# A perceiver block on one core: the first stage's tiles in a new order

## The reference, cut to what matters

```python
x = x + xattn0(layernorm(x), ctx)      # (gelu_tanh(xn ctx^T) * (xn ctx^T)) ctx
x = x + attn0(layernorm(x))            # qkv; RMS norm of q and k per head; rotation; causal softmax, 16 heads of 32
x = x + experts(layernorm(x))          # 32 experts, top 2 of a softmax, capacity 77, hidden 2048
x = x + xattn1(layernorm(x), ctx)      # 16 heads over 257 keys
x = x + attn1(layernorm(x))            # decayed attention, group norms, silu feed-forward
x = x + spectral(layernorm(x))         # fft -> product with w -> real ifft, + bias

def _rms_norm(t, w):
    return t * rsqrt(mean(t * t) + EPS) * w
# _rope(q, k): [q1*cos - q2*sin, q2*cos + q1*sin] of the normed q and k
```

## Time and profile before

| | us |
|---|---|
| runs, median of 3 | 2064.54 (2060.41 to 2065.12) |
| the profiled execution: time | 2075.67 |
| its span | 2073.9 |
| PE busy | 1934.6 (93%) |
| DVE, ACT, POOL busy | 704.7, 556.9, 196.9 |
| mean granted clock of TensorE | 0.97 |
| first stage with its routing, to the experts' first product | 336.55 |

### The profile page before, as it was taken

The page is one execution under the profiler, slowest core; times in us unless marked ns, Lnnn a source line. Parts: engine busy times, 40 slices in busy tenths (PEclk is TensorE's granted clock), DMA queues, the critical chain, the costliest instruction groups (busy, mean ns, idle before and its releaser), DMA issues.

```text
span 2073.9 us, 37462 instructions
## 1 busy us (share of the span) xinstructions
PE 1934.6 (93%) x15676; PEld 981.9 (47%) x15676; DVE 704.7 (34%) x1536; ACT 556.9 (27%) x1123; POOL 196.9 (9%) x182
## 2 busy tenths in 40 slices
PE   5789777999999999999996999999999999999977
PEld 2444453333333333333333657565666656575543
DVE  2666671121111211112223433434323333344323
ACT  1333311222222222222211234233333333242321
POOL 1122221000000000000003000000000000000000
PEclk9999988999999999999998999999999999999988
DMA  9643228999999999999976020100000000000000
GB/s 338 221 163 144 79 73 344 396 396 387 382 388 375 380 362 379 379 375 379 367 280 207 22 102 22 27 21 27 12 26 22 21 27 22 17 22 27 11 1 11
DMA packets 86295, 374.95 MB, mean 181 GB/s; under 512 B 7782, under 2 KB 25702, under 8 KB 53432
## 3 DMA queue, kind: packets, MB, share of 16 engines
q1 hardware_dynamic: 79544, 355.71, 44.9%
q0 software_dynamic: 6656, 17.77, 2.4%
HBM read 357.73 MB, written 16.45 MB: 180 GB/s over the span
## 4 chain that ended last, share of the span: by engine, by line
PE 85%; issue 4%; ACT 3%; SPq 3%; DMA 2%; DVE 2%; POOL 1%; another core or an unknown queue 0%; POOLq 0%; DVEq 0%; ACTq 0%
PE ps L1323 38%; PE ps L1506 16%; PE ps L1488 16%; PE ps L1713 3%; PE ps L1496 2%; PE ps L1608 1%; PE ps L1514 1%; DMA arena<-in_ctxT 1%; ACT arena L685 1%; PE ps L1384 1%; PE ps L1593 1%; DMA xe_rows<-arena,uidx 1%; PE ps L1634 1%; SPq L432 1%; PE ps L1477 1%
## 5 line engine op out<-in xcount | busy, mean ns | idle before, releaser
L1323 PE MATMUL ps<-arena 128*128 128x512 f32 (+3 forms) x3120 | 893.6, 442 | 38.0 <-ACT arena L685 10.0
L1323 PEld LDWEIGHTS ps<-arena 128*128 128x128 f32 x3120 | 529.1, 193 | 372.6 <-issue 296.7
L1506 PE MATMUL ps<-arena 128*32 128x512 f32 x3072 | 373.6, 594 | 0.0
L1488 PE MATMUL ps<-arena 128*32 128x512 f32 x3072 | 363.3, 595 | 0.7 <-issue 0.6
L550 POOL TENSOR_TENSOR arena<-arena 128x1 f32<-128x1 f32 (+3 forms) x80 | 129.2, 1615 | 1103.2 <-DVE arena L913 643.7
L1121 DVE COPY arena<-ps 128x512 f32<-128x512 f32 x96 | 66.4, 691 | 482.7 <-PE ps L1506 482.7
L1488 PEld LDWEIGHTS ps<-arena 128*32 128x32 f32 x3072 | 109.3, 109 | 225.4 <-issue 225.4
L1506 PEld LDWEIGHTS ps<-arena 128*32 128x32 f32 x3072 | 100.4, 109 | 198.1 <-issue 195.6
L783 ACT ACTIVATE arena<-ps 128x512 f32<-128x512 f32 x96 | 57.3, 597 | 352.5 <-PE ps L1488 352.5
L813 ACT ACTIVATE arena<-ps,arena 128x257 f32<-128x257 f32 x128 | 60.7, 477 | 202.8 <-PE ps L1323 202.8
L1220 DVE TENSOR_REDUCE arena<-ps 128x1 f32<-128x257 f32 x128 | 54.2, 423 | 122.5 <-PE ps L1593 112.7
(11 more groups left out here) (198 smaller groups left out, 1323.8 us busy)
## 6 DMA issues: line engine op xcount, KB each, us to landing
arena<-in_w SPq DMA_DIRECT2D x64, 4096.0 KB, 13.8
arena<-in_ctxT SPq DMA_DIRECT2D x8, 2056.0 KB, 7.9
arena<-in_ctxT SPq DMA_DIRECT2D x32, 514.0 KB, 3.6
arena<-in_ctx SPq DMA_DIRECT2D x8, 2048.0 KB
xe_rows<-arena SPq DMA_DIRECT2D x8, 616.0 KB
arena<-in_b POOLq DMA_DIRECT2D x32, 154.0 KB, 7.5
arena<-xe_rows SPq DMA_DIRECT2D x32, 154.0 KB
y_rows<-arena POOLq DMA_DIRECT2D x32, 154.0 KB, 6.2
```

The lines of the kernel that those rows point to most:

```text
L1323: ins = pe.matmul(dst, lhsT, rhs, start=(n == 0), stop=(n == len(pairs) - 1))
L1488: ins = pe.matmul(ps[q4[n], t, :], xeT[s][:, k, q4[t]], w1_sb[s][:, k, n * D:(n + 1) * D], start=(k == 0), stop=(k == KD - 1))
L1506: ins = pe.matmul(ps[q4[n], ST + t, :], hT[s][:, t, c, q4[n]], w2_sb[s][:, n * HB + c, :], start=(c == 0), stop=(c == HB - 1))
```

## The change

A new piece generator, `lead(i)` (letter h), takes norm 0 and its transposes and copy out of `gated(i)`; it runs two tiles ahead of `scored` and one ahead of `gated`, and tile 1's stands ahead of `scored(0)`. Norm 1 is cut into `moments` and `normed`, in two pieces. On DVE the rotation reads the products in PSUM (banks 4 and 5) and is multiplied by the root afterwards (into qkr); the buffer qkn now holds the rotated values. On PE the QKV product is issued values first, then a `yield`, then queries and keys; the scores move from `scored(i)` to the first piece of `attended(i)`, so that they stand in the next turn between its value product and its query and key products. The transposed queries and keys now lie in banks 4 and 5, the scores in bank 3 (6 for the last tile, function bA), transposes of xn and the logits in bank 3 (7 for the last two, bR). The loop runs over i = 2 to 5 and tile 6's turn is written out behind it. The folds are cut in halves, one behind the last rotation, one ahead of the last softmax. The pieces of ACT and POOL follow. Line numbers here are those of the changed kernel where the order rows show them.

```diff
 
-        PLAN_A = "gzawgawgzgagzaga"
-        PLAN_B = "zwwrmrzzrm"
+        PLAN_A = "hazagawzgawgzagazh"
+        PLAN_B = "wzwrmrzzzrm"
         CUT = NT - 2
...
             if isinstance(i, int) and i == tile:
                 eng.wait_ge(s, value)
 
+        def bA(i):
+            return 6 if isinstance(i, int) and i == NT - 1 else 3
+
+        def bR(i):
+            return 7 if isinstance(i, int) and i >= NT - 2 else 3
+
         def counts_at(part):
             a, b = BATCHES[part]
             return 2 * a * E, (a + b) * E, 2 * b * E
 
-        def phase_a(eng, gated, scored, attended, routed, spectral, my, per, route):
-
+        def phase_a(eng, lead, gated, scored, attended, routed, spectral, my, per, route):
+
+            run(lead(0))
             run(gated(0))
-            interleave(PLAN_A, a=scored(0), g=gated(1))
-            interleave(PLAN_A, a=scored(1), g=gated(2), z=attended(0))
-            with eng.Fori(2, NT - 1) as i:
+            run(lead(1))
+            interleave(PLAN_A, a=scored(0), g=gated(1), h=lead(2))
+            interleave(PLAN_A, a=scored(1), g=gated(2), h=lead(3), z=attended(0))
+            with eng.Fori(2, NT - 2) as i:
                 if my is not None:
                     my.loop(i, per, 2)
-                interleave(PLAN_A, a=scored(i), g=gated(i + 1), z=attended(i - 1), w=routed(i - 2))
+                interleave(PLAN_A, a=scored(i), g=gated(i + 1), h=lead(i + 2), z=attended(i - 1), w=routed(i - 2))
             if my is not None:
-                my.leave(NT - 1)
+                my.leave(NT - 2)
+            interleave(PLAN_A, a=scored(NT - 2), g=gated(NT - 1), z=attended(NT - 3), w=routed(NT - 4))
             interleave(PLAN_A, a=scored(NT - 1), z=attended(NT - 2), w=routed(NT - 3))
             interleave(PLAN_B, z=attended(NT - 1), w=routed(NT - 2), m=spectral, r=route(0))
             run(routed(NT - 1))
...
             def norm_root(a, n):
                 root(veps, rstd, ln_stats[a], n + 1, ln_rstd[a])
 
+            def lead(i):
+                norm_root(0, i)
+                yield
+                yield
+
             def gated(i):
-                norm_root(0, i)
-                yield
-                yield
                 yield
                 yield
                 norm_root(1, i)
...
             def bc(ap, *shape):
                 return ap.broadcast_to(list(shape))
 
-            def layer_norm(a, src, dst, n, done=None, w=None):
-                stats_rdy, rstd_rdy = (ln_stats[a], ln_rstd[a]) if w is None else (w.ln_stats, w.ln_rstd)
+            def moments(a, src, w=None):
+                stats_rdy = ln_stats[a] if w is None else w.ln_stats
                 dve.drain()
                 dve.bn_stats(stats, src)
                 dve.drain()
                 my.step(dve.bn_aggr(mv, stats))
                 TS(veps, mv[:, 1:2], LN_EPS, None, ALU.add).then_inc(stats_rdy, 1)
+
+            def normed(a, src, dst, n, done=None, w=None):
+                rstd_rdy = ln_rstd[a] if w is None else w.ln_rstd
                 dve.wait_ge(rstd_rdy, n + 1)
                 ins = TS(dst, src, mv[:, 0:1], rstd, ALU.subtract, ALU.mult)
                 if done is None:
                 else:
                     ins.then_inc(done, 1)
 
+            def layer_norm(a, src, dst, n, done=None, w=None):
...
                     return a[:, i, :]
                 return a[:, bass.ds(i, 1), :].rearrange("p a d -> p (a d)")
 
+            def lead(i):
+                first_at(dve, i, 1, x_in, 16)
+                moments(0, tile_of(x_sb, i))
+                wait(dve, xT_ps[0], i)
+                normed(0, tile_of(x_sb, i), xn0, i, xn_rdy[0])
+                yield
+                yield
+
             def gated(i):
                 xt = tile_of(x_sb, i)
-                first_at(dve, i, 1, x_in, 16)
-                layer_norm(0, xt, xn0, i, xn_rdy[0])
-                yield
-                yield
                 dve.wait_ge(g_rdy, i + 1)
                 TT(hA, g_sb, ps[:, 1, 0:S], ALU.mult).then_inc(hA_rdy, 1)
                 yield
                 yield
                 dve.wait_ge(gated_ps, i + 1)
                 TT(xt, xt, ps[:, 2, :], ALU.add)
-                layer_norm(1, xt, xn1, i, xn_rdy[1])
-                yield
-                yield
-
-            def folds():
-                for even, odd, w, w_in in ((We_r, Wo_r, Wr_sb, Wr_in), (We_i, Wo_i, Wi_sb, Wi_in)):
-                    dve.wait_ge(w_in, 16)
-                    TT(even[:, :, 1:HF], w[:, :, 1:HF], w[:, :, D - 1:HF:-1], ALU.add).then_inc(W_fold, 1)
-                    TT(odd[:, :, 1:HF], w[:, :, 1:HF], w[:, :, D - 1:HF:-1], ALU.subtract).then_inc(W_fold, 1)
-                    dve.tensor_copy(even[:, :, 0:1], w[:, :, 0:1]).then_inc(W_fold, 1)
-                for odd, other, sign in ((Wo_r, Wi_sb, 1.0), (Wo_i, Wr_sb, -1.0)):
-                    TS(odd[:, :, 0:1], other[:, :, HF:HF + 1], sign, None, ALU.mult).then_inc(W_fold, 1)
+                moments(1, xt)
+                yield
+                normed(1, xt, xn1, i, xn_rdy[1])
+                yield
+
+            def folds(part):
+                even, odd, w, w_in = ((We_r, Wo_r, Wr_sb, Wr_in), (We_i, Wo_i, Wi_sb, Wi_in))[part]
+                dve.wait_ge(w_in, 16)
+                TT(even[:, :, 1:HF], w[:, :, 1:HF], w[:, :, D - 1:HF:-1], ALU.add).then_inc(W_fold, 1)
+                TT(odd[:, :, 1:HF], w[:, :, 1:HF], w[:, :, D - 1:HF:-1], ALU.subtract).then_inc(W_fold, 1)
...
                 dve.wait_ge(sq_rdy, i + 1)
                 my.step(dve.reduce_sum(ms, sq, AX.X))
                 TS(ms, ms, 1.0 / DH, RMS_EPS, ALU.mult, ALU.add).then_inc(ms_rdy, 1)
-                if isinstance(i, int) and i == NT - 1:
-                    folds()
-                yield
-                dve.wait_ge(rs_rdy, i + 1)
-                my.step(TT(qkn, ps[:, 4:6, :].rearrange("p a (h d) -> p (a h) d", h=H),
-                           bc(rs.unsqueeze(2), P, 2 * H, DH), ALU.mult))
+                yield
                 v4 = "p (a h) d -> p a h d"
-                qn4, A4, B4 = (a.rearrange(v4, a=2) for a in (qkn, ropeA, ropeB))
+                A4, B4 = (a.rearrange(v4, a=2) for a in (ropeA, ropeB))
+                qn4 = ps[:, 4:6, :].rearrange("p a (h d) -> p a h d", h=H)
                 my.step(TT(A4, qn4, bc(CW.unsqueeze(2), P, 2, H, DH), ALU.mult))
                 hd = DH // 2
                 my.step(TT(B4[:, :, :, 0:hd], qn4[:, :, :, hd:DH],
                            bc(SW[:, :, 0:hd].unsqueeze(2), P, 2, H, hd), ALU.mult))
                 my.step(TT(B4[:, :, :, hd:DH], qn4[:, :, :, 0:hd],
                            bc(SW[:, :, hd:DH].unsqueeze(2), P, 2, H, hd), ALU.mult))
-                TT(qkr, ropeA, ropeB, ALU.add).then_inc(qkr_rdy, 1)
-                yield
+                my.step(TT(qkn, ropeA, ropeB, ALU.add))
+                if isinstance(i, int) and i == NT - 1:
+                    folds(0)
+                yield
+                yield
+                dve.wait_ge(rs_rdy, i + 1)
+                TT(qkr, qkn, bc(rs.unsqueeze(2), P, 2 * H, DH), ALU.mult).then_inc(qkr_rdy, 1)
                 yield
                 yield
 
...
                 xt = tile_of(x_sb, i)
 
                 first_at(dve, i, 0, consts_in, 16 * N_CONST)
+                if isinstance(i, int) and i == NT - 1:
+                    folds(1)
                 dve.wait_ge(s_ps, i + 1)
...
 
             def spectral():
                 pe.wait_ge(W_fold, 8)
+                pe.wait_ge(lg_rdy, NT - 2)
                 pe.wait_ge(dft_in, 16 * 2)
                 spectral_chunk(0)
                 yield
...
 
             pe.wait_ge(id_in, 16)
 
-            def gated(i):
+            def lead(i):
                 yield
                 pe.wait_ge(xn_rdy[0], i + 1)
                 for k in range(KD):
                     ins = pe.transpose(ps[:, 0, chunk(k)], xn0[:, k:D:KD], id_sb)
                 ins.then_inc(xT_ps[0], 1)
                 yield
+
...
                                         start=(j == 0), stop=(j == SJ - 1))
                 ins.then_inc(gated_ps, 1)
                 yield
-                wait(pe, qkT_rdy, 5 * i - 4)
+                wait(pe, lg_rdy, i - 2)
                 transposes(1, xn1, i, 3)
                 yield
 
             def scored(i):
                 pe.wait_ge(xT_rdy[1], i + 1)
                 first_at(pe, i, 0, wA_in, 16 * WA)
-                for a in range(3):
+                wait(pe, vA_rdy, i)
+                for a in (2, 0, 1):
+                    group(ps[:, 4 + a, :], [(xnT[:, k, :], wqkv0_sb[:, k, a * D:(a + 1) * D]) for k in range(KD)],
+                          qkv_ps if a == 1 else None)
                     if a == 2:
-                        wait(pe, sA_rdy, i)
-                    group(ps[:, 4 + a, :], [(xnT[:, k, :], wqkv0_sb[:, k, a * D:(a + 1) * D]) for k in range(KD)],
-                          qkv_ps if a == 2 else None)
+                        yield
+                yield
```

(19 more changed lines are left out.)

33 lines of the change are left out of this document (20 added, 13 removed).

## The result

| us | before | after |
|---|---|---|
| median of the runs (20 each) | 2062.88 (2059.38 to 2070.68) | 2055.49 (2051.09 to 2059.27) |
| after to before | | 0.9962, 95% interval 0.9955 to 0.9969 |
| the profiled execution: time, span | 2075.67, 2073.9 | 2057.88, 2056.3 |

The kernel is faster by 7.4 us, 0.4%; forecast were 25.2. So the sign was right, and the time lies 4.5 us above the range. The question is where some 18 us of the expected gain went.

A forecast was written before the change was run, and what follows sets the result against it. The prediction took PE, busy 93% of the span, as the bound, with the first stage setting the experts' start. Terms -24.2 + 2.9 - 3.9 = -25.2 took the 2064.5 median to about 2039.5 us, range 2031 to 2051.

The forecast's parts named there:

- Nothing outside this stage is edited, so what counts is how much earlier 336.55 comes: First stage: only an earlier first product of the experts, at 336.55 us before, counts; forecast 25.2 us in all.
- rival 4: Experts' start: held by something else, such as weights or landing of scatters, so time stays 2064; chance 0.02.
- Term 1: First stage's tile loop: PE's waits go and a tile takes 25.6 us; six periods fall from 176.5 to 152.3, -24.2.
- Term 2: First stage's start: QKV(0) waits for tile 1's transposes, so the loop's pace begins at 78.2, not 75.32: +2.9.
- Term 3: First stage's end: last query and key product to first scatter shrinks from 45.3 to 41.4 us, -3.9.
- E: The end of a tile's query and key products, from which the forecast counted its times.
- all behind follows: First stage's end: after softmax at 23.7, not 27.6, everything to the first scatter moves along, reaching it at 41.4.
- The wait at xn1: First stage's loop: PE newly waits 0.2 to 0.3 us for DVE before xn1's transposes.
- Rivals 1 to 3: 1: lower clock or longer tiles, +8, 0.23; 2: DVE bounds, +14, 0.08; 3: PE's loop clock stays low, 2094, 0.03.
- Rival 5: First stage: start without loss and work at full clock throughout, giving 2032 us; chance 0.05.
- ACT's table load: First stage's gelu: switch costs 1.28 us without the skill's 1.38 drain, which would make the sum some 4.5 worse.
- Scatters to experts: From first scatter to the experts' first product: the distance stays at 39.5 us.

The follow-up runs named there:

- The pads: Kernels with unused one-column products added on PE to shift the last loop's code; for example, 35 of them in the changed kernel: 2041.68 us.
- after_pad16: The changed kernel with 4 unused one-column products (16 PE instructions) between the first stage and the experts: 2057.84 us, ratio to before 0.997.
- after_pad40: The changed kernel with 10 unused one-column products (40 PE instructions) in the first stage: 2042.54 us, ratio to before 0.9887.
- rotation_after_root: The changed kernel with 18 unused one-column products, and DVE's rotation put back behind its wait for the large root: 2080.2 us, ratio to before 1.0069.
- ctxT_ahead_of_zeros: Changed kernel plus 18 short products, earlier first-tile QKV, xn1 before the root multiplication, and third tile's ctxT and ctx loads before the zero stores: 2031.2 us, ratio 0.983.

## Why the prediction was wrong, point by point

- **The step that failed** is the sentence "Nothing outside this stage is edited, so what counts is how much earlier 336.55 comes". 336.55 came 24.1 us earlier, and 17.6 us were lost over five turns of a loop whose source is untouched but whose place in PE's list had moved by 372 instructions. The prediction put the change of all that stands behind the stage at nothing, because no line of it is edited. No rival had it either: rival 4 looked for what else could hold the experts' start, and none looked behind it. The pads show the cause.
- **Term 1, the tiles, -24.2**: 152.3 from 77.75 to 230.08, against 176.5, is -24.2. A tile took 25.5 (25.6 forecast), at clock 1.00.
- **Term 2, the start, +2.9**: 77.75 against 75.32, +2.4. QKV(0) started at 36.00, near the 36.3 walked. That the term fits is in part luck: in the seven padded kernels made from the changed one, with the same first stage, the place lies between 73.93 (after_pad16) and 78.43 (after_pad40), beside a granted clock of 0.94 and 0.76 between 50 and 78 us.
- **Term 3, the end, -3.9**: from the last query and key product to the first scatter (273.08) it is 43.0 against 45.3, so -2.3. The granted clock, 0.80 against 0.81, is not what took the rest. The walk holds through softmax (E + 23.3, walked 23.7) and the routing on DVE, which ends 4.7 us earlier counted from E. What failed is "all behind follows": the addition ahead of tile 7's norm now waits 2.5 us on DVE for PE's projection, where before it followed the routing with 0.04 between (now, then before). The three sum to -24.1.

```profile
270.13 0.69 DVE L1036 TENSOR_TENSOR arena<-arena,ps 128x512 f32<-128x512 f32 x1 [2.47 <-PE ps L1356]
```

```profile
294.11 0.69 DVE L1003 TENSOR_TENSOR arena<-arena,ps 128x512 f32<-128x512 f32 x1
```

- **The wait at xn1** was forecast at 0.2 to 0.3 and is 0.7. The step took the small root as hidden below the multiplication; but the root took 1.46 and not 0.55 there and ended 0.41 behind it. That the tile came out all the same means that its work was somewhat below 25.2: PE is busy 24.8.
- **Rivals 1 to 3**: the clock did not stay down in the loop and DVE did not become its bound. The nearest to either is rotation_after_root, where DVE is late and the clock falls: a tile of 30.6. Rival 5, more than forecast, needed the start without loss; ctxT_ahead_of_zeros, another kernel, shows such a start.
- **ACT's table load**: no drain of 1.38 us is seen. In the loop the squares end at 129.56, a load of 1.28 starts at 129.58 and the gelu at 130.87, and the tile is not longer. The figure of the Trainium skill (ScalarE: Activation LUTs, What ACT_TABLE_LOAD costs) isn't borne out here, and the row was the right choice.
- **Scatters to experts**: forecast unchanged at 39.5, measured 39.4.

## What to carry to other kernels

An edit to one part of an engine's list moves all that comes behind it. After an edit that adds or removes instructions ahead of a hot hardware loop, compare the loop's turns in the two traces first, and look for idle time put down to "issue" at the head of a turn. If it is there, a few idle instructions ahead of the loop, at a place where the engine stands anyway, cost little and can be worth more than the edit: here 10 to 35 short products gave 13 to 16.5 us by the medians, where the edit alone gave 7.4. How many are needed can be read from one trace: the instructions between the loop's start and the gap are those that the block still had, 16 here, and a padding somewhat longer moves the start behind the border. One that is just as long is the worst place (after_pad16). And when a wait is taken away, look at what it hid: here the order of loads was the next bound at 75 us, and moving one tile's loads was worth 5.

## What the hardware did that was not expected

- A loop's turn cost some 3.5 us more by the place of its first instruction alone, 17.6 us over five turns in the changed kernel; the kernel before lost 20.4 in all by the same place. The Trainium skill (Runtime: NRT & Kernel Launch, Instruction fetch mechanics) has the blocks and the stall at a branch, and puts the crossing of a border at mostly hidden. The traces agree on the 16 KB packets and for most borders of a turn, and show one that is not hidden when it is met 0 to 68 instructions behind the place to which the loop jumps back; at 132 it is.
- DVE's multiplication of two operands from SBUF (1.21 us) held POOL's root of 128 x 1 up: 1.46 us beside it, 0.55 without. Beside DVE operations that read PSUM it stayed at 0.55 (150.84, in rotation_after_root). The Trainium skill (Advanced Engine Details and Errata, GPSIMD Details) says that POOL conflicts with DVE instructions that have two inputs in SBUF: the trace agrees where DVE's operation was the first to run. The other way round nothing is seen: the rotation's addition, two inputs from SBUF, took its 1.23 while the large root ran (108.81, beside 105.59 to 111.02), and the root took its 5.43, as in the kernel before.
